# Quantising the output weights inside the loop of the first FFN product instead of after it (selective scan and ternary FFN, 8 cores)

## Chip, cores and metric

One Trainium2 chip, 8 cores. Each core runs the same program on one of the 8 batch elements, and the cores exchange nothing. The metric is device time in microseconds (us) of the slowest core; lower is better.

## What is computed

Per batch element (sequence S = 2048, width D = 2048, hidden width H = 8192), cut to what matters:

```python
x = layernorm(x + selective_scan_ffn(x, ...))
# ternary ("bit") FFN
h  = x * rsqrt(mean(x*x) + EPS) * w_norm
gv = act_quant(h) @ weight_quant(w_gv).T          # w_gv: 2*H x D
value, gate = split(gv)
u  = value * silu(gate)
out = act_quant(u) @ weight_quant(w_out).T        # w_out: D x H
x = layernorm(x + (x + out))

def weight_quant(w):                              # ternary: -1, 0, 1
    scale = 1.0 / max(mean(abs(w)), EPS)
    return clip(round(w * scale), -1, 1) / scale
def act_quant(x):                                 # 8 bits, one scale for each token
    scale = 127 / max(max(abs(x), axis=-1), EPS)
    return clip(round(x * scale), -128, 127) / scale
```

## The kernel before, in words

The program is a row of stages, each written as separate functions for the engines. Every compute instruction of VectorE (DVE) and ScalarE (ACT) goes through a wrapper (`SyncEng`, line 80 in the profile for all of them): it raises the engine's own semaphore (`sV` for DVE, `sA` for ACT), and the engine waits for that count before its next instruction. So each of the two engines runs strictly one instruction after the other, and all waits across engines are waits on these counts. `TOK` holds the counts, worked out ahead by loops that repeat the order of the code.

The stages, in order: the selective scan with the mean of all weights beside it; a stage that makes the quantised activations `q1`, kept in SBUF; **F1**, the product with `w_gv`; the **wo stage**, which quantises `w_out`; **F15**, which turns the running maximum `Mx` of |u| into per-token scales; then quantising `u` (`zt`, `mq`) and the product with the quantised `w_out` (line 1348).

**F1** (lines 957 to 1060) loops over j = 0..63 blocks of 128 hidden units. In step j:

- SyncE (SP) loads the value and the gate block of the weights (1 MB each, `wld`, ring of 3) a step ahead.
- ACT makes |w·s| into `wqt` and sign(w·s) into `wqs`, DVE combines them into ternary bf16 weights, `qwv` for the value block, and the same once more into `qwg` for the gate block. I call these four ACT and two DVE instructions the *quantising part*.
- TensorE (PE) multiplies: 4 slices of 512 tokens, 16 + 16 matmuls for each slice, into `pvg`. It waits for `qwg` of step j and, slice by slice, for `u` of step j-1, which frees PSUM.
- For step j-1, four times (once for each slice): DVE `gc_t` = gate·c1b, ACT `sg_t` = silu(gc_t), DVE `sg_t`·c1b, DVE `u_r` = value·sg_t, ACT `au_t` = |u_r|, DVE `Mx` = max(Mx, au_t). I call it the *epilogue*. After the fourth, ACT issues the store of `u_r` (1 MB, `u_sp`) on its own DMA queue.

**The wo stage** (lines 1062 to 1110) starts when F1 has ended. 128 units of 128x1024 weights: SP loads `wo_r` (512 KB, 2 buffers), ACT makes |w·s| and sign(w·s) into the first halves of `wqt` and `wqs`, DVE combines them into `qo_t` (2 buffers), ACT issues the store of unit i-1 to `qo_sp` (256 KB). The next unit's first ACT instruction waits for the DVE instruction of this one, since `wqt` is single.

After it F15 begins on DVE with a copy `trt` from `Mx`. The loads of `u_sp` by GpSimd (POOL) and of `qo_sp` by SP further on wait for the stores.

Of the kernel before, what the change touches and what calls it, by code (L numbers as in the profile page):

```python
# [86 lines left out]
def build_program(upto="F2", dbg=()):  # L87
    stage_n = STAGES.index(upto) - 4
    nc = bass.Bass("TRN2", target_bir_lowering=False)
# [15 lines left out]
    woutT = nc.dram_tensor("woutT", [2, HC, 128, 8 * 128], F32, kind="ExternalInput").ap()  # L105
# [4 lines left out]
    qo_sp = nc.dram_tensor("qo_sp", [2, HC // 4, 128, 4 * 1024], BF16, kind="Internal").ap()  # L110
# [789 lines left out]
    u_r = fsb(nc.sbuf_tensor("u_r", [128, 2 * S], F32))  # L900
    gc_t = fsb(nc.sbuf_tensor("gc_t", [128, TS], F32))
    sg_t = fsb(nc.sbuf_tensor("sg_t", [128, TS], F32))
    au_t = fsb(nc.sbuf_tensor("au_t", [128, TS], F32))
    wo_r = fsb(nc.sbuf_tensor("wo_r", [128, 2 * 1024], F32))
    qo_t = fsb(nc.sbuf_tensor("qo_t", [128, 2 * 1024], BF16))
    f1p = contextlib.ExitStack()
    pvg = f1p.enter_context(nc.psum_tensor("pvg", [128, 8 * TS], F32))

# [15 lines left out]
    for j in range(HC + 1):  # L924
        if j < HC:
            a += 2; TOK[("qv", j)] = a
            a += 2; TOK[("qg", j)] = a
        if j >= 1:
            jj = j - 1
            for ts in range(NTS):  # L930
                a += 1; TOK[("silu", jj, ts)] = a
                a += 1; TOK[("au", jj, ts)] = a
            _usp_cnt[jj % 2] += 16
            TOK[("usp", jj)] = (rUSP.sems[jj % 2].h, _usp_cnt[jj % 2])
    for j in range(HC + 1):
        if j < HC:
            v_ += 1; TOK[("ternv", j)] = v_
            v_ += 1; TOK[("terng", j)] = v_
        if j >= 1:
            jj = j - 1  # L940
            for ts in range(NTS):
                v_ += 1; TOK[("gc", jj, ts)] = v_
                v_ += 1; TOK[("sg2", jj, ts)] = v_
                v_ += 1; TOK[("u", jj, ts)] = v_
                v_ += 1; TOK[("mx", jj, ts)] = v_
    for j in range(HC):
        for ts in range(NTS):
            m += 1
            TOK[("mm", j, ts)] = m
# [21 lines left out]
    @SCA  # L971
    def _(sc):
        sc.wait_ge(sA.h, tok_w0done)
        for j in range(HC + 1):
            if j < HC:
                sc.wait_ge(*TOK[("ldv", j)])
                if j >= 1:
                    sc.wait_ge(sV.h, TOK[("terng", j - 1)])
                sc.activation(out=wqt[:], in_=wld[:, (2 * j % 3) * 2048:(2 * j % 3 + 1) * 2048],
                              func=AF.Abs, scale=sgv128[:])  # L980
                sc.activation(out=wqs[:], in_=wld[:, (2 * j % 3) * 2048:(2 * j % 3 + 1) * 2048],
                                     func=AF.Sign, scale=sgv128[:])
                sc.wait_ge(*TOK[("ldg", j)])
                sc.wait_ge(sV.h, TOK[("ternv", j)])
                sc.activation(out=wqt[:], in_=wld[:, ((2 * j + 1) % 3) * 2048:((2 * j + 1) % 3 + 1) * 2048],
                              func=AF.Abs, scale=sgv128[:])
                sc.activation(out=wqs[:], in_=wld[:, ((2 * j + 1) % 3) * 2048:((2 * j + 1) % 3 + 1) * 2048],
                                     func=AF.Sign, scale=sgv128[:])
            if j >= 1:
                jj = j - 1  # L990
                r = jj % 2
                for ts in range(NTS):
                    sc.wait_ge(sV.h, TOK[("gc", jj, ts)])
                    sc.activation(out=sg_t[:], in_=gc_t[:], func=AF.Silu)
                    sc.wait_ge(sV.h, TOK[("u", jj, ts)])
                    sc.activation(out=au_t[:],
                                         in_=u_r[:, r * S + ts * TS:r * S + (ts + 1) * TS],
                                         func=AF.Abs)
                sc.wait_ge(sV.h, TOK[("mx", jj, NTS - 1)])
                rUSP.inc(jj, sc.dma_start(out=u_sp[jj], in_=u_r[:, r * S:(r + 1) * S]))  # L1000
    assert sA.n == end_a

    @VEC
    def _(v):
        for j in range(HC + 1):
            if j < HC:
                v.wait_ge(sA.h, TOK[("qv", j)])
                if j >= 2:
                    v.wait_ge(sMM.h, TOK[("mm", j - 2, NTS - 1)])
                v.scalar_tensor_tensor(  # L1010
                    out=qwv[:, (j % 2) * 2048:(j % 2 + 1) * 2048], in0=wqt[:],
                    scalar=0.5, in1=wqs[:], op0=ALU.is_ge, op1=ALU.mult)
                v.wait_ge(sA.h, TOK[("qg", j)])
                v.scalar_tensor_tensor(
                    out=qwg[:, (j % 2) * 2048:(j % 2 + 1) * 2048], in0=wqt[:],
                    scalar=0.5, in1=wqs[:], op0=ALU.is_ge, op1=ALU.mult)
            if j >= 1:
                jj = j - 1
                r = jj % 2
                for ts in range(NTS):  # L1020
                    q = (jj * NTS + ts) % 4
                    v.wait_ge(sMM.h, TOK[("mm", jj, ts)])
                    v.tensor_mul(out=gc_t[:],
                                 in0=pvg[:, (2 * q + 1) * TS:(2 * q + 2) * TS],
                                 in1=c1b[:, ts * TS:(ts + 1) * TS])
                    v.wait_ge(sA.h, TOK[("silu", jj, ts)])
                    v.tensor_mul(out=sg_t[:], in0=sg_t[:],
                                 in1=c1b[:, ts * TS:(ts + 1) * TS])
                    if jj >= 2:
                        v.wait_ge(*TOK[("usp", jj - 2)])  # L1030
# [43 lines left out]
    @SCA
    def _(sc):
        for i in range(2 * HC + 1):
            if i < 2 * HC:
                sc.wait_ge(rWO.sems[i % 2].h, 16 * (i // 2 + 1))
                if i == 0:
                    sc.wait_ge(sV.h, wo_v0)  # L1080
                else:
                    sc.wait_ge(sV.h, wo_v0 + i)
                sc.activation(out=wqt[:, 0:1024],
                              in_=wo_r[:, (i % 2) * 1024:(i % 2 + 1) * 1024],
                              func=AF.Abs, scale=sout128[:])
                sc.activation(out=wqs[:, 0:1024],
                              in_=wo_r[:, (i % 2) * 1024:(i % 2 + 1) * 1024],
                              func=AF.Sign, scale=sout128[:])
            if i >= 1:
                ii = i - 1  # L1090
                dg, j = divmod(ii, HC)
                sc.wait_ge(sV.h, wo_v0 + ii + 1)
                rQoS.inc(ii, sc.dma_start(
                    out=qo_sp[dg, j // 4, :, (j % 4) * 1024:(j % 4 + 1) * 1024],
                    in_=qo_t[:, (ii % 2) * 1024:(ii % 2 + 1) * 1024]))
    tok_woq = sA.n

    @VEC
    def _(v):
        for i in range(2 * HC):  # L1100
            v.wait_ge(sA.h, wo_a0 + 2 * (i + 1))
            if i >= 2:
                v.wait_ge(rQoS.sems[i % 2].h, 16 * (i // 2))
            v.scalar_tensor_tensor(out=qo_t[:, (i % 2) * 1024:(i % 2 + 1) * 1024],
                                   in0=wqt[:, 0:1024], scalar=0.5,
                                   in1=wqs[:, 0:1024], op0=ALU.is_ge, op1=ALU.mult)
    tok_qodone = sV.n
# [466 lines left out]
```

## Time and profile before

| | us |
|---|---|
| median of 2 runs (7633.83 and 7651.46) | 7642.64 |
| the profiled execution, its time | 7636.9 |
| its span on the slowest core (core 0) | 7635.3 |
| spans of all cores | 7598.5 to 7635.3 |
| busy in that span: PE, DVE, ACT, POOL | 3231.7, 4178.1, 3082.2, 247.8 |
| mean granted TensorE clock, cores 0 to 7 | 0.697 to 0.701 |

The profile covers one execution, on its slowest core. "PE" is TensorE's matmuls, "SPq", "ACTq" and "POOLq" are the parts of an engine that issue DMAs. Times inside it are counted from the span's start.

### The profile page before, as it was taken

What the parts mean: (1) busy time and instruction counts of PE and PEld (TensorE: products, weight loads), DVE (VectorE), ACT (ScalarE), POOL (GpSimd) and SP (SyncE); (2) the same over time, 40 slices, a digit from 0 to 9 for tenths busy, and PEclk for the clock granted to TensorE, in tenths of its full rate; (3) what the DMA queues carried; (4) which work ended last, traced back from release to release, by engine and by line L of the source; (5) the groups of instructions that cost most, each with busy time, mean ns of one, the idle gap of its engine ahead of it and who ended that gap; (6) DMA issues with size and microseconds to landing.
All of it is one profiled execution on the core that took longest, in us unless ns stands there. A gap on an engine that the chain in (4) does not pass through costs nothing.

```text
span 7635.3 us, 48837 instructions; the slowest of 8 cores (7598.5 to 7635.3 us)
## 1 busy us (share of the span) xinstructions
PE 3231.7 (42%) x12882; PEld 1326.2 (17%) x13138; DVE 4178.1 (55%) x3305; ACT 3082.2 (40%) x2971; POOL 247.8 (3%) x471
## 2 busy tenths in 40 slices
PE   2200202102088888888888100000540714426186
PEld 0000000000033333333333000000220202112032
DVE  3845374665844444444444334677776576576612
ACT  2520212122143443344333554566565465465501
POOL 2011000000000000000000000000000000000000
PEclk8555555555599999999999555555775857668577
DMA  8998200001032222222222565111434415325233
GB/s 187 318 332 257 70 14 31 22 22 41 0 110 94 100 94 94 94 100 94 94 94 89 172 197 165 50 59 63 152 109 137 135 52 176 94 99 165 67 121 110
DMA packets 217459, 853.69 MB, mean 112 GB/s; under 512 B 34656, under 2 KB 34656, under 8 KB 159840
## 3 DMA queue, kind: packets, MB, share of 16 engines
q1 hardware_dynamic: 101808, 503.38, 20.2%
q0 software_dynamic: 50864, 179.37, 8.3%
q10 hardware_dynamic: 64512, 167.80, 5.9%
q8 instruction: 108, 1.77, 0.1%
q14 instruction: 167, 1.37, 0.1%
HBM read 694.24 MB, written 167.77 MB: 113 GB/s over the span
## 4 chain that ended last, share of the span: by engine, by line
DVE 49%; ACT 18%; DMA 14%; PE 7%; issue 7%; ACTq 2%; POOL 2%; DVEq 1%; POOLq 0%; SPq 0%
DVE zt L80 16%; DMA ub<-u_sp 5%; ACT wqt L80 5%; ACT wqs L80 5%; DVE res L80 3%; DVE paby L80 3%; PE pout L1348 3%; DMA wmean<-wgvt 3%; DVE Mx L80 3%; DVE sg_t L80 2%; DVE gc_t L80 2%; DVE u_r L80 2%; DMA wo_r<-woutT 2%; ACT sg_t L80 2%; ACT au_t L80 2%
## 5 line engine op out<-in xcount | busy, mean ns | idle before, releaser
L1348 PE MATMUL pout<-q_r,qo_r 128*128 128x512 bf16 x4012 | 935.4, 394 | 1127.4 <-DMA qo_r<-qo_sp 588.7
L1050 PE MATMUL pvg<-q,qwv 128*128 128x512 bf16 x4014 | 1025.4, 410 | 381.2 <-DVE u_r L80 215.9
L80 DVE SCALAR_TENSOR_TENSOR zt<-mq,zt 128x1024 f32<-128x1024 f32 x896 | 1098.7, 1226 | 160.4 <-DVE zt L80 158.2
L80 ACT ACTIVATE mq<-zt,pbh 128x1024 f32<-128x1024 f32 x896 | 1028.8, 1148 | 229.8 <-DVE zt L80 226.7
L1055 PE MATMUL pvg<-q,qwg 128*128 128x512 bf16 x4014 | 919.9, 379 | 4.3
L80 ACT ACT_TABLE_LOAD x82 | 105.2, 1283 | 1712.0 <-DVE q L80 404.3
L1348 PEld LDWEIGHTS pout<-q_r,qo_r 128*128 128x128 bf16 x4096 | 410.9, 101 | 1656.2 <-issue 1257.9
L1050 PEld LDWEIGHTS pvg<-q,qwv 128*128 128x128 bf16 x4096 | 422.6, 104 | 954.5 <-issue 547.8
L1055 PEld LDWEIGHTS pvg<-q,qwg 128*128 128x128 bf16 x4096 | 400.8, 98 | 483.3
L80 DVE TENSOR_TENSOR ub<-ub,s2b 128x1024 f32<-128x1024 f32 x128 | 156.9, 1225 | 435.4 <-DMA ub<-u_sp 434.5
L80 ACT ACTIVATE sg_t<-gc_t 128x512 f32<-128x512 f32 x256 | 161.2, 630 | 552.4 <-DVE gc_t L80 552.4
L80 ACT ACTIVATE wqt<-wld,sgv 128x2048 f32<-128x2048 f32 x128 | 256.3, 2002 | 251.7 <-DVE qwv L80 164.6
L80 DVE SCALAR_TENSOR_TENSOR qo_t<-wqt,wqs 128x1024 bf16<-128x1024 f32 x128 | 156.9, 1226 | 354.5 <-ACT wqs L80 332.7
L80 ACT ACTIVATE au_t<-u_r 128x512 f32<-128x512 f32 x256 | 161.2, 630 | 469.5 <-DVE u_r L80 469.5
L80 DVE TENSOR_REDUCE accW<-wmean 128x1 f32<-128x2048 f32 (+1 forms) x128 | 224.4, 1753 | 212.2 <-DMA wmean<-wgvt 144.8
L1233 POOL DMA_DIRECT2D ub<-u_sp x256 | 136.2, 536 | 6242.0 <-ACT c2b L80 4024.9
L80 DVE SCALAR_TENSOR_TENSOR qwv<-wqt,wqs 128x2048 bf16<-128x2048 f32 x64 | 146.7, 2293 | 313.8 <-ACT wqs L80 308.9
L80 ACT ACTIVATE wabs<-wmean 128x2048 f32<-128x2048 f32 (+1 forms) x128 | 189.9, 1483 | 283.1 <-DMA wmean<-woutT 204.7
L1448 PE MATMUL pout<-o_ts,onesc 128*1 128x512 f32 x128 | 63.9, 663 | 567.6 <-DVE o_ts L80 567.6
L80 ACT ACTIVATE mq<-ub,pbh 128x1024 f32<-128x1024 f32 x128 | 147.0, 1148 | 378.2 <-DVE ub L80 377.0
L80 DVE SCALAR_TENSOR_TENSOR qwg<-wqt,wqs 128x2048 bf16<-128x2048 f32 x64 | 146.7, 2292 | 275.3 <-ACT wqs L80 275.3
L80 DVE TENSOR_TENSOR Mx<-Mx,au_t 128x512 f32<-128x512 f32 x256 | 177.2, 692 | 212.7 <-ACT au_t L80 212.7
(147 smaller groups left out, 3682.1 us busy)
## 6 DMA issues: line engine op xcount, KB each, us to landing
wld<-wgvt SPq DMA_DIRECT2D x128, 1024.0 KB, 5.5
qo_r<-qo_sp SPq DMA_DIRECT2D x128, 1024.0 KB, 5.7
wmean<-wgvt SPq DMA_DIRECT2D x64, 1024.0 KB, 7.6
wmean<-wgvt POOLq DMA_DIRECT2D x64, 1024.0 KB, 11.3
u_sp<-u_r ACTq DMA_DIRECT2D x64, 1024.0 KB, 4.1
wo_r<-woutT SPq DMA_DIRECT2D x128, 512.0 KB, 3.8
ub<-u_sp POOLq DMA_DIRECT2D x256, 256.0 KB, 5.5
wmean<-woutT SPq DMA_DIRECT2D x64, 512.0 KB, 12.8
```

What stands on the lines that cost most here:

```text
L80: r = f(*a, **kw)
L1050: t.matmul(pvg[:, 2 * q * TS:(2 * q + 1) * TS], qwv[:, r * 2048 + k * 128:r * 2048 + (k + 1) * 128], q1[:, (ts * DC + k) * TS:(ts * DC + k ...
L1055: last = t.matmul(pvg[:, (2 * q + 1) * TS:(2 * q + 2) * TS], qwg[:, r * 2048 + k * 128:r * 2048 + (k + 1) * 128], q1[:, (ts * DC + k) * TS ...
L1233: tk = rUB.inc(u, g.dma_start(out=ub2[:, (2 * lane + half) * TS:(2 * lane + half + 1) * TS], in_=u_sp[2 * u + half, :, ts * TS:(ts + 1) * ...
L1348: last = t.matmul(pout[:, d * TS:(d + 1) * TS], qo_r[:, base + d * 128:base + (d + 1) * 128], rhs, start=(j == 0), stop=(j == HC - 1))
L1448: sMM.inc(t.matmul(pout[0:1, 0:TS], onesc[:], o_ts[:, d * TS:(d + 1) * TS], start=(d == 0), stop=(d == DC - 1)))
```

## The change

The wo stage as a stage of its own is gone. Its 128 units now run inside F1's loop, two per step, behind the epilogue (and in step 0, where there is no epilogue, behind the quantising part). `au_t` is dropped: |u| is written into `gc_t`, whose silu has been taken by then. The freed room and more goes to `woqt` and `woqs`, the units' own buffers for |w·s| and the sign. The loads of `wo_r` move from SP to GpSimd. On ACT the store of unit i-2 is issued ahead of unit i; the last two stores follow the last epilogue. The waits now go by `TOK`.

```diff
-    au_t = fsb(nc.sbuf_tensor("au_t", [128, TS], F32))
     wo_r = fsb(nc.sbuf_tensor("wo_r", [128, 2 * 1024], F32))
     qo_t = fsb(nc.sbuf_tensor("qo_t", [128, 2 * 1024], BF16))
+    woqt = fsb(nc.sbuf_tensor("woqt", [128, 1024], F32))
+    woqs = fsb(nc.sbuf_tensor("woqs", [128, 1024], BF16))
...
@@ ACT, loop over j, in the epilogue
-                    sc.activation(out=au_t[:],
+                    sc.activation(out=gc_t[:],
                                          in_=u_r[:, r * S + ts * TS:r * S + (ts + 1) * TS],
                                          func=AF.Abs)
                 sc.wait_ge(sV.h, TOK[("mx", jj, NTS - 1)])
                 rUSP.inc(jj, sc.dma_start(out=u_sp[jj], in_=u_r[:, r * S:(r + 1) * S]))
+            for h in ((0, 1) if j < HC else ()):
+                i = 2 * j + h
+                wl = i % 2
+                if i >= 2:
+                    sc.wait_ge(sV.h, TOK[("wot", i - 2)])
+                    dgp, jwp = divmod(i - 2, HC)
+                    rQoS.inc(i - 2, sc.dma_start(
+                        out=qo_sp[dgp, jwp // 4, :, (jwp % 4) * 1024:(jwp % 4 + 1) * 1024],
+                        in_=qo_t[:, wl * 1024:(wl + 1) * 1024]))
+                sc.wait_ge(rWO.sems[wl].h, 16 * (i // 2 + 1))
+                if i >= 1:
+                    sc.wait_ge(sV.h, TOK[("wot", i - 1)])
+                sc.activation(out=woqt[:],
+                              in_=wo_r[:, wl * 1024:(wl + 1) * 1024],
+                              func=AF.Abs, scale=sout128[:])
+                sc.activation(out=woqs[:],
+                              in_=wo_r[:, wl * 1024:(wl + 1) * 1024],
+                              func=AF.Sign, scale=sout128[:])
+            if j == HC:
+                for i in (2 * HC - 2, 2 * HC - 1):
...
@@ DVE, loop over j
                     v.tensor_max(out=Mx[:, ts * TS:(ts + 1) * TS],
-                                 in0=Mx[:, ts * TS:(ts + 1) * TS], in1=au_t[:])
+                                 in0=Mx[:, ts * TS:(ts + 1) * TS], in1=gc_t[:])
+            for h in ((0, 1) if j < HC else ()):
+                i = 2 * j + h
+                wl = i % 2
+                v.wait_ge(sA.h, TOK[("woq", i)])
+                if i >= 2:
+                    v.wait_ge(rQoS.sems[wl].h, 16 * (i // 2))
+                v.scalar_tensor_tensor(out=qo_t[:, wl * 1024:(wl + 1) * 1024],
+                                       in0=woqt[:], scalar=0.5, in1=woqs[:],
+                                       op0=ALU.is_ge, op1=ALU.mult)
...
-    wo_a0 = sA.n
-    wo_v0 = sV.n
-
-    @blk.sync
-    def _(s):
+    @blk.gpsimd
+    def _(g):
         for i in range(2 * HC):
-            if i >= 2:
-                s.wait_ge(sV.h, wo_v0 + (i - 1))
-            dg, j = divmod(i, HC)
-            rWO.inc(i, s.dma_start(out=wo_r[:, (i % 2) * 1024:(i % 2 + 1) * 1024],
-                                   in_=woutT[dg, j]))
...
+            if i < 2:
+                g.wait_ge(sV.h, pP_v)
+                g.wait_ge(sA.h, pP_a)
+                g.wait_ge(sLn1.h, tok_ln1_all)
+            else:
+                g.wait_ge(sA.h, TOK[("woq", i - 2)])
+            dg, jw = divmod(i, HC)
+            rWO.inc(i, g.dma_start(out=wo_r[:, (i % 2) * 1024:(i % 2 + 1) * 1024],
+                                   in_=woutT[dg, jw]))
```

Left out is the removed code of the wo stage on ACT and DVE, which is told in words above.

ACT before, end of an F1 step and start of the next (the DMA is the store of `u_r`):

```order
L80 ACTIVATE sg_t<-gc_t 128x512 [waits sA,sV]
L80 ACTIVATE au_t<-u_r 128x512 [waits sA,sV]
L1000 DMA u_sp<-u_r 128x2048 [waits sA,sV]
L80 ACTIVATE wqt<-wld,sgv 128x2048 [waits rWLD0,sV]
L80 ACTIVATE wqs<-wld,sgv 128x2048 [waits sA]
```

ACT now, at the same place (`rWO` are the semaphores of the `wo_r` loads):

```order
L80 ACTIVATE sg_t<-gc_t 128x512 [waits sA,sV]
L80 ACTIVATE gc_t<-u_r 128x512 [waits sA,sV]
L1007 DMA u_sp<-u_r 128x2048 [waits sA,sV]
L1014 DMA qo_sp<-qo_t 128x1024 [waits sV]
L80 ACTIVATE woqt<-wo_r,sout 128x1024 [waits rWO0,sV]
L80 ACTIVATE woqs<-wo_r,sout 128x1024 [waits sA]
L1014 DMA qo_sp<-qo_t 128x1024 [waits sA,sV]
L80 ACTIVATE woqt<-wo_r,sout 128x1024 [waits rWO1,sV]
L80 ACTIVATE woqs<-wo_r,sout 128x1024 [waits sA]
L80 ACTIVATE wqt<-wld,sgv 128x2048 [waits sA,rWLD2,sV]
```

Four activations and two stores stand between the store of `u_r` and the next quantising part; the first `qo_sp` store is directly behind the `u_sp` store on the same queue.

DVE before, the same place:

```order
L80 TENSOR_TENSOR u_r<-pvg,sg_t 128x512 [waits sV,rUSP1,sA]
L80 TENSOR_TENSOR Mx<-Mx,au_t 128x512 [waits sV,sA]
L80 SCALAR_TENSOR_TENSOR qwv<-wqt,wqs 128x2048 [waits sV,sA,sMM]
L80 SCALAR_TENSOR_TENSOR qwg<-wqt,wqs 128x2048 [waits sV,sA]
L80 TENSOR_TENSOR gc_t<-pvg,c1b 128x512 [waits sV,sMM]
```

DVE now (`rQoS` are the semaphores of the `qo_sp` stores):

```order
L80 TENSOR_TENSOR u_r<-pvg,sg_t 128x512 [waits sV,rUSP0,sA]
L80 TENSOR_TENSOR Mx<-Mx,gc_t 128x512 [waits sV,sA]
L80 SCALAR_TENSOR_TENSOR qo_t<-woqt,woqs 128x1024 [waits sV,sA,rQoS0]
L80 SCALAR_TENSOR_TENSOR qo_t<-woqt,woqs 128x1024 [waits sV,sA,rQoS1]
L80 SCALAR_TENSOR_TENSOR qwv<-wqt,wqs 128x2048 [waits sV,sA,sMM]
L80 SCALAR_TENSOR_TENSOR qwg<-wqt,wqs 128x2048 [waits sV,sA]
L80 TENSOR_TENSOR gc_t<-pvg,c1b 128x512 [waits sV,sMM]
```

Two DVE instructions were put in, each with a wait for the store of the unit that used its half of `qo_t` before.

## Rows read from the trace of the kernel before

**Rows 1.** F1 and wo stage: us, then PE, PEld, DVE, ACT, POOL busy, PEclk, DMA, GB/s

```profile
2102.00:4152.00 2050.00, 1812.04 (x7752) 795.75 (x7912) 964.04 (x1102) 809.35 (x740) 0.00 (x0) 0.94 0.27 97
4232.00:4742.00 510.00, 0.00 (x0) 0.00 (x0) 157.12 (x129) 293.69 (x257) 0.00 (x0) 0.50 0.63 196
```

**Rows 2.** Chain of waits over one step of F1 (start us, us, what)

```profile
3016.53 0.70 DVE Mx L80
3017.30 0.33 ACTq L1000
...
3017.79 2.01 ACT wqt L80
...
3031.11 0.70 DVE gc_t L80
...
3035.94 0.70 DVE gc_t L80
...
3049.92 0.70 DVE Mx L80
```

**Rows 3.** First quantising instruction of steps 2 and 63, timeline of ACT

```profile
2155.99 2.00 ACT L80 ACTIVATE wqt<-wld,sgv 128x2048 f32<-128x2048 f32 x1 [1.36 <-DVE Mx L80]
...
4178.05 2.00 ACT L80 ACTIVATE wqt<-wld,sgv 128x2048 f32<-128x2048 f32 x1 [1.36 <-DVE Mx L80]
```

**Rows 4.** The wo stage's two ends, timeline

```profile
4229.51 0.69 DVE L80 TENSOR_TENSOR Mx<-Mx,au_t 128x512 f32<-128x512 f32 x1 [0.82 <-ACT au_t L80]
...
4741.79 1.22 DVE L80 COPY trt<-Mx 64x2048 f32<-64x2048 f32 x1 [0.17 <-DVE qo_t L80]
```

**Rows 5.** One unit of the wo stage, timeline

```profile
4255.68 1.15 ACT L80 ACTIVATE wqt<-wo_r,sout 128x1024 f32<-128x1024 f32 x1 [1.49 <-DVE qo_t L80]
4256.92 1.15 ACT L80 ACTIVATE wqs<-wo_r,sout 128x1024 bf16<-128x1024 f32 x1
...
4258.24 1.23 DVE L80 SCALAR_TENSOR_TENSOR qo_t<-wqt,wqs 128x1024 bf16<-128x1024 f32 x1 [2.65 <-ACT wqs L80]
4259.56 1.15 ACT L80 ACTIVATE wqt<-wo_r,sout 128x1024 f32<-128x1024 f32 x1 [1.49 <-DVE qo_t L80]
```

**Rows 6.** DMA issues of the page: engine, count, KB each, median us to landing

```profile
wmean<-wgvt POOLq DMA_DIRECT2D x64, 1024.0 KB, 11.3
u_sp<-u_r ACTq DMA_DIRECT2D x64, 1024.0 KB, 4.1
```

**Rows 7.** DMA traffic 3017 to 3023 us (one `u_sp` store), in 40 slices

```profile
GB/s 0 0 0 0 0 0 0 492 382 382 492 382 492 273 601 273 601 55 819 0 765 109 655 218 0 0 0 0 0 0 0 0 0 0 0 0 0 0 0 0
```

**Rows 8.** DMA traffic 4740 to 4748 us (two `qo_sp` stores), in 40 slices

```profile
GB/s 0 0 0 0 0 51 338 389 399 133 0 0 102 410 369 369 62 0 0 0 0 0 0 0 0 0 0 0 0 0 0 0 0 0 0 0 0 0 0 0
qo_sp<-qo_t ACTq DMA_DIRECT2D x2, 256.0 KB, 2.4
```

**Rows 9.** Sixteen 256 KB stores in a row on ACT's queue, timeline

```profile
891.79 9.98 ACTq L716 DMA_DIRECT2D ln_sp<-res  x16
```

**Rows 10.** `qo_t` and its stores, 4599 to 4612 us: DMA to landing

```profile
DMA to landing us min/median/max: 3.8/4.0/4.0
```

**Rows 11.** Step 0 and 1 of F1 on ACT, timeline

```profile
2117.17 2.00 ACT L80 ACTIVATE wqs<-wld,sgv 128x2048 bf16<-128x2048 f32 x1
2121.66 2.00 ACT L80 ACTIVATE wqt<-wld,sgv 128x2048 f32<-128x2048 f32 x1 [2.49 <-DVE qwg L80]
...
2145.35 0.63 ACT L80 ACTIVATE sg_t<-gc_t 128x512 f32<-128x512 f32 x1 [1.75 <-DVE gc_t L80]
...
2151.68 0.63 ACT L80 ACTIVATE sg_t<-gc_t 128x512 f32<-128x512 f32 x1 [3.39 <-DVE gc_t L80]
```

**Rows 12.** PE in F1 and after a long idle stretch, timeline

```profile
2238.12 6.42 PE L1050 MATMUL pvg<-q,qwv 128*128 128x512 bf16 x16 [4.45 <-DVE u_r L80]
...
3016.85 3.62 PE L1050 MATMUL pvg<-q,qwv 128*128 128x512 bf16 x16
...
5630.16 29.57 PE L1348 MATMUL pout<-q_r,qo_r 128*128 128x512 bf16 x126 [149.62 <-ACT o_ts L80]
```

More of the change, by code:

```diff
@@ L934, in build_program @@
             TOK[("usp", jj)] = (rUSP.sems[jj % 2].h, _usp_cnt[jj % 2])
+        if j < HC:
+            for h in (0, 1):
+                a += 2; TOK[("woq", 2 * j + h)] = a
     for j in range(HC + 1):
@@ L945, in build_program @@
                 v_ += 1; TOK[("mx", jj, ts)] = v_
+        if j < HC:
+            v_ += 1; TOK[("wot", 2 * j)] = v_
+            v_ += 1; TOK[("wot", 2 * j + 1)] = v_
     for j in range(HC):
@@ L1000, in _ @@
                 rUSP.inc(jj, sc.dma_start(out=u_sp[jj], in_=u_r[:, r * S:(r + 1) * S]))
+            for h in ((0, 1) if j < HC else ()):
[19 more added lines that the diff above has]
+                    wl = i % 2
+                    sc.wait_ge(sV.h, TOK[("wot", i)])
+                    dgp, jwp = divmod(i, HC)
+                    rQoS.inc(i, sc.dma_start(
+                        out=qo_sp[dgp, jwp // 4, :, (jwp % 4) * 1024:(jwp % 4 + 1) * 1024],
+                        in_=qo_t[:, wl * 1024:(wl + 1) * 1024]))
     assert sA.n == end_a
@@ L1036, in _ @@
                     v.tensor_max(out=Mx[:, ts * TS:(ts + 1) * TS],
-                                 in0=Mx[:, ts * TS:(ts + 1) * TS], in1=au_t[:])
+                                 in0=Mx[:, ts * TS:(ts + 1) * TS], in1=gc_t[:])
+            for h in ((0, 1) if j < HC else ()):
+                i = 2 * j + h
+                wl = i % 2
+                v.wait_ge(sA.h, TOK[("woq", i)])
[4 more added lines that the diff above has]
+                                       op0=ALU.is_ge, op1=ALU.mult)
     assert sV.n == end_v
@@ L1060, in build_program @@
     assert sMM.n == end_m
-    wo_a0 = sA.n
-    wo_v0 = sV.n
-    @blk.sync
-    def _(s):
+    @blk.gpsimd
+    def _(g):
         for i in range(2 * HC):
-            if i >= 2:
-                s.wait_ge(sV.h, wo_v0 + (i - 1))
-            dg, j = divmod(i, HC)
-            rWO.inc(i, s.dma_start(out=wo_r[:, (i % 2) * 1024:(i % 2 + 1) * 1024],
-                                   in_=woutT[dg, j]))
[L1074 to L1107, printed above, removed]
+            if i < 2:
[7 more added lines that the diff above has]
+                                   in_=woutT[dg, jw]))
+    tok_woq = end_a
+    tok_qodone = end_v
     tok_qosp = [s.tok() for s in rQoS.sems]
```

## Prediction

> **What bounds the kernel now.** I read first how busy each engine is by stage [rows 1]. In F1 no engine is full: of 2050 us PE works 1812, DVE 964 and ACT 809. DVE and ACT together make 1773, so the question is whether they ever work side by side. The chain of waits over one step says that they don't: the step goes from the end of `Mx` at 3016.53 + 0.69 = 3017.22 over the store's issue to `wqt` at 3017.79, and then in turns between ACT and DVE through the quantising part up to 3031.1 and through four epilogues of about 4.83 us each (3031.11 to 3035.94) to the next `Mx` at 3049.92 [rows 2]. PE is not in it. From step 2 to step 63 the first `wqt` moves from 2155.99 to 4178.05, 61 steps, or 33.15 us a step [rows 3]. So F1 is bounded by one chain of ACT and DVE in turns; all that is put into it lengthens it.
>
> The wo stage is such a chain too. PE does nothing there, and of 510 us ACT works 294 and DVE 157 [rows 1]. A unit starts with ACT at 4255.68, its sign at 4256.92, DVE at 4258.24, and the next unit's ACT at 4259.56: 3.88 us [rows 5]. From the last `Mx` of F1 (4229.51 + 0.69 = 4230.20) to the first copy of F15 at 4741.79 it is 511.6 us for 128 units, 4.0 each [rows 4].
>
> **What is removed.** F15 starts 0.17 us behind the last DVE instruction of F1 instead of behind the last unit [rows 4]. That takes 511.6 - 0.2 = 511.4 us away. What comes later (F15, the quantising of `u`, the second product) has the same work. The last two `qo_sp` stores are issued right ahead of F15 as they were before, so what waits for them further on waits for nothing new.
>
> **What is put into the step.** The units stand between the epilogue and the next quantising part on both engines, so they are on the chain, and PE's idle time doesn't help, since PE was never what they waited for. I follow one step from `Mx`'s end at 3017.22, with the durations of rows 5.
>
> 1. The `u_sp` store is issued at 3017.30 for 0.33 us as before [rows 2]. The `qo_sp` store of unit i-2 follows. Sixteen stores in a row took 9.98 us to issue, 0.62 each [rows 9]; I take 0.5, between 0.33 for one alone and that. ACT starts the first unit at 3018.3 instead of 3017.79.
> 2. DVE could start 2.56 us later (4255.68 to 4258.24 [rows 5]), at 3020.86.
> 3. But DVE now also waits for the `qo_sp` store just issued, as it will overwrite that half of `qo_t`. That is the term which the change doesn't show. Alone it would be there in time: 2.4 us to landing [rows 8], so 3017.7 + 2.4 = 3020.1. Yet it stands behind 1 MB of `u_sp` on one queue. The traffic of such a store begins 0.75 us after the issue and lasts until about 3020.6 (slices 8 to 24 of 0.15 us, 3018.05 to 3020.6 [rows 7]), and it lands 4.1 us after issue, at 3021.4 [rows 6]. The 256 KB behind it need some 0.7 us more: the first of two such stores filled about four slices of 0.2 us [rows 8], and 16 in a row took 0.62 each [rows 9]. Both have the same 0.8 us from the last byte to landing (rows 6 and 7: 3021.4 less 3020.6). So it lands at about 3022.1, and DVE starts at 3022.15, a wait of 1.3 us.
> 4. ACT's second unit starts 1.32 us after DVE did (4258.24 to 4259.56 [rows 5]), at 3023.47. Its store was issued right behind the first sign, and has landed before it is asked for. ACT goes on to `wqt` of the next step after twice 1.24 us (4255.68 to 4256.92 [rows 5]), at 3025.95. It doesn't wait for DVE here, for `woqt` and `woqs` are buffers of their own, and DVE's second 1.23 us lie beside the 4.2 us of `wqt` and `wqs`.
>
> The step grows by 3025.95 - 3017.79 = 8.16 us. Without the wait in 3 it would be 1.29 less, 6.87.
>
> A rule of the Trainium skill speaks to this wait (DMA: Bandwidth & Descriptors, "Queues, rings and completion order"): descriptors of a queue are consumed in ring order on each DMA engine, and the write that raises the semaphore lands only after all earlier writes of that engine. By it the small store can't overtake the large one and the wait stands; a store that overtook it would give the 6.87 above. No row of before has a `qo_sp` store behind a `u_sp` store, so the trace doesn't decide it.
>
> **The first and the last step.** In step 0 the two units stand behind the quantising part: the last sign starts at 2117.17 and is over at about 2119.26, then abs and sign, DVE at 2121.8, the second pair from 2123.1, and step 1 starts at 2125.6 instead of 2121.66 [rows 11], 4.0 late. The first epilogue there lost some 1.6 us to PE (ACT idle 3.39 ahead of the `sg_t` at 2151.68, against 1.75 a slice earlier [rows 11]), which falls away: +2.4. In step 63 no quantising part follows, and DVE's second unit comes onto the chain: it starts 2.56 after 3023.47 and ends 1.4 later with its gap, so the next `gc_t` comes at 3027.43 instead of 3017.39: +10.0.
>
> **Sum.** 62 × 8.16 + 2.4 + 10.0 - 511.4 = 505.9 + 12.4 - 511.4 = +6.9 us. From the profiled execution, 7636.9, that is 7644 us, against a median of 7642.64 for the runs shown: no change.
>
> **What I cost at nothing, and its cover.** `gc_t` in the place of `au_t` adds no wait: on both engines the reader is through before the next writer, by the engine's own order. GpSimd has nothing else to do in F1 [rows 1]; its load of unit i+2 is issued when ACT is through with unit i, and is wanted a step later, over 33 us, while loads of twice the size from there took 11.3 us in the crowded first stage [rows 6]. If that cover went, ACT would stand still at the head of a unit. PE has 8 groups of 16 matmuls a step, at most 3.62 us each [rows 12], 29.0 us, in a step that grows to 41.3. It may start slower after the longer idle time, and I bound this from both sides: nothing, as in the group of 3.62, and 2.8 us, as in the group of 6.42 behind 4.45 us idle. Behind 149.6 us idle, 126 matmuls took 29.57 us, where 7.9 groups of 3.62 are 28.5, about 1 us more [rows 12]. All that stays below 32, so PE isn't on the chain.
>
> **Rivals.**
>
> *A: the small store isn't held up* (by the large one, or since engines that finish early serve it first). For it: only the receipt at the end is shared. Against: the DMA slices are full of the large store until 3020.6 [rows 7], and both are on one queue. A step grows by 6.87, and 63 steps give back 81 us: 7563.
>
> *B, slower: the small store starts only when the large one has landed, or lands late.* The place is DVE's wait for `rQoS` in front of the first unit. For it: where the stage was crowded, such a store took 4.0 us instead of 2.4 [rows 10]. Against: 16 in a row kept the queue going at 0.62 us each [rows 9]. With landing at 3021.4 + 2.4 = 3023.8 DVE starts 1.7 us later than I say, 63 × 1.7 = 107 us: 7751. With 3021.4 + 4.0 = 3025.4 it is 3.3 us, 208 us: 7852. From any delay on the result is on the slower side, as the forecast sum is just above zero, and it is over 2% from 2.3 us of delay on (146 us over 63 steps).
>
> *C: PE falls behind since it stays at its lower level.* At 1.2 instead of 2.4 GHz a step of PE is 58 us, more than 41.3, and F1 would end 62 × (58 - 41.3) = 1035 us later than by my sum: some 8680. It decides from where PE needs over 41.3 us, with some 40% of its matmuls at the lower level. For it: the granted clock was 0.94 of full in F1 with 4 us idle a step (2050 - 1812 over 62 steps, rows 1), and now there are 11. Against: after 149.6 us idle the loss was 1 us and then over [rows 12]. The Trainium skill warns of it (TensorE: Matmul & The Clock Gate, "HAM oscillation"): idle stretches between bursts make each burst start throttled. That rule and the row agree on a cost for each burst; by it C would not come, as each burst here is 128 matmuls long.
>
> *D: the units cost less than rows 5 say*, 5.6 us or less a step, over 2% faster. The chain of four ACT and one DVE instruction alone is 2.56 + 1.32 + 2.48 = 6.36 us [rows 5], so almost nothing is for it.
>
> **Chances.** My forecast 0.60 (its own range 7612 to 7676, from 0.5 us of error a step either way); A 0.20; B 0.15, a third of it over 2%; C 0.03; D 0.02. The predicted time is 7644. The range reaches to A and to the nearer end of B: 7560 to 7750. 2%, about what a measurement of this kernel can tell from no change, is 153 us. Faster by over 2%: 0.03. Slower: 0.05 from B and 0.03 from C, 0.08. Within: 0.89.
>
> **What would show it.** In the new profile: the distance between two first `wqt` is 41.3 us from step 2 on; in the waits DVE `qo_t` is released by the DMA `qo_sp<-qo_t` once a step, with about 1.3 us behind ACT's sign; the `qo_sp` stores have two kinds of landing, some 4.4 and some 2.4 us; no ACT instruction waits for `wo_r`; PE's idle time in front of a step is some 11 us and its first group 5 to 6.5; F15 starts 0.2 us behind the last `Mx`, at about 4749. I am wrong in the main term if DVE starts the first unit before 3.8 us or after 6 us past `Mx`'s end, and wrong in kind if PE or a `wo_r` load ends a wait in F1.

## The result and the profile after

The changed kernel takes 7664.36 us (median of 33 runs, 7626.77 to 7707.91), the kernel before beside it 7633.3 us (32 runs). The ratio is 1.0041, 95% interval 1.0027 to 1.0055: about 31 us slower, within 2%. Forecast were +7 us and no change.

The profiled execution's slowest core is core 5, with a span of 7684.7 us; the others range from 7605.0 to 7677.2. The places of [rows 3] and [rows 4], in the timeline of that core (start us, us, engine, line, operation; in brackets the idle time before and what ended it):

```profile
2102.07 2.00 ACT L80 ACTIVATE wqt<-wld,sgv 128x2048 f32<-128x2048 f32 x1
2160.11 2.00 ACT L80 ACTIVATE wqt<-wld,sgv 128x2048 f32<-128x2048 f32 x1 [0.20 <-ACT woqs L80]
4707.45 2.00 ACT L80 ACTIVATE wqt<-wld,sgv 128x2048 f32<-128x2048 f32 x1 [0.20 <-ACT woqs L80]
4769.08 0.69 DVE L80 TENSOR_TENSOR Mx<-Mx,gc_t 128x512 f32<-128x512 f32 x1 [0.82 <-ACT gc_t L80]
4769.94 1.22 DVE L80 COPY trt<-Mx 64x2048 f32<-64x2048 f32 x1 [0.17 <-DVE Mx L80]
```

The wo stage is gone: `trt` starts 0.17 us behind the last `Mx`, where it was 511.6 us [rows 4]. Steps 2 to 63 now take (4707.45 - 2160.11) / 61 = 41.76 us each, against 33.15 [rows 3]: 8.61 more. Where the 8.61 go is seen in one step, the stretch of [rows 2]:

```profile
3030.00 0.69 DVE L80 TENSOR_TENSOR Mx<-Mx,gc_t 128x512 f32<-128x512 f32 x1 [0.83 <-ACT gc_t L80]
...
3030.77 0.33 ACTq L1007 DMA_DIRECT2D u_sp<-u_r  x1
3031.18 0.40 ACTq L1014 DMA_DIRECT2D qo_sp<-qo_t  x1
3031.74 1.15 ACT L80 ACTIVATE woqt<-wo_r,sout 128x1024 f32<-128x1024 f32 x1 [1.84 <-issue]
3032.98 1.15 ACT L80 ACTIVATE woqs<-wo_r,sout 128x1024 bf16<-128x1024 f32 x1
...
3034.26 0.33 ACTq L1014 DMA_DIRECT2D qo_sp<-qo_t  x1
...
3035.80 1.22 DVE L80 SCALAR_TENSOR_TENSOR qo_t<-woqt,woqs 128x1024 bf16<-128x1024 f32 x1 [5.11 <-DMA qo_sp<-qo_t]
...
3037.12 1.15 ACT L80 ACTIVATE woqt<-wo_r,sout 128x1024 f32<-128x1024 f32 x1 [3.00 <-DVE qo_t L80]
3038.36 1.15 ACT L80 ACTIVATE woqs<-wo_r,sout 128x1024 bf16<-128x1024 f32 x1
3039.68 1.23 DVE L80 SCALAR_TENSOR_TENSOR qo_t<-woqt,woqs 128x1024 bf16<-128x1024 f32 x1 [2.66 <-ACT woqs L80]
3039.71 2.00 ACT L80 ACTIVATE wqt<-wld,sgv 128x2048 f32<-128x2048 f32 x1 [0.20 <-ACT woqs L80]
```

The sign of the first unit ends at 3034.13, but DVE starts at 3035.80, when the store issued at 3031.18 has landed. The second unit's DVE instruction lies beside `wqt`, and no ACT instruction waits for a `wo_r` load. The waits of DVE for `qo_t`, over the whole program (us in total, times), and the landing of the `qo_sp` stores:

```profile
  DMA qo_sp<-qo_t: 330.1, 63
  ACT woqs L80: 170.4, 65
...
DMA to landing us min/median/max: 2.3/4.4/6.2
```

The median landing is over two kinds of store: those directly behind `u_sp` land 4.5 us after their issue, the others 2.8 (medians of each kind). The 330.1 us are the whole idle time from the last `Mx` to the start of the first unit's DVE instruction, 63 times 5.24 us (5.07 in the median step, 6.75 in the longest). And PE, in the rows that answer to [rows 12]:

```profile
3056.32 6.56 PE L1092 MATMUL pvg<-q,qwv 128*128 128x512 bf16 x16 [12.19 <-DVE u_r L80]
```

It stands idle for 12.19 us ahead of a step, where it was 4.45 in [rows 12], and its first group of 16 is slow as it was there: the granted clock is 0.54 in it, nearly all at its lower level (1.2 GHz, 0.5), and 1.00 (2.4 GHz) in the group that starts at 3033.61. PE costs the chain nothing: six waits of DVE for `qwv` are put down to PE, 18.7 us in total, but they last 3.1 us each, as when ACT ends them (3.07).

### The profile page after: what moved, and what is told of

Its sections match the earlier page's. It is cut to its first block, busy times and chain, and to the rows that moved or that the text cites. A ratio compares the mean times of both kernels' runs of the same rounds, so it can differ in the third digit from the quotient of the medians.

```text
span 7684.7 us, 49097 instructions; the slowest of 8 cores (7605.0 to 7684.7 us)
## 1 busy us (share of the span) xinstructions
PE 3373.7 (44%) x13138; PEld 1353.6 (18%) x13138; DVE 4177.8 (54%) x3305; ACT 3081.0 (40%) x2970; POOL 315.4 (4%) x599
## 4 chain that ended last, share of the span: by engine, by line
DVE 49%; ACT 17%; DMA 15%; PE 8%; issue 7%; POOL 2%; ACTq 1%; DVEq 1%; POOLq 0%; SPq 0%
DVE zt L80 16%; DMA ub<-u_sp 5%; DMA qo_sp<-qo_t 4%; PE pout L1358 3%; DVE res L80 3%; ACT wqt L80 3%; ACT wqs L80 3%; DVE paby L80 3%; DMA wmean<-wgvt 3%; DVE Mx L80 3%; DVE sg_t L80 2%; DVE u_r L80 2%; DVE gc_t L80 2%; ACT sg_t L80 2%; ACT gc_t L80 2%
## 5 line engine op out<-in xcount | busy, mean ns | idle before, releaser
L1358 PE MATMUL pout<-q_r,qo_r 128*128 128x512 bf16 x4096 | 1013.7, 417 | 1086.7 <-DMA qo_r<-qo_sp 570.9
L1092 PE MATMUL pvg<-q,qwv 128*128 128x512 bf16 x4096 | 1069.4, 421 | 864.9 <-DVE u_r L80 705.5
L1097 PE MATMUL pvg<-q,qwg 128*128 128x512 bf16 x4096 | 937.1, 382 | 0.0
L1358 PEld LDWEIGHTS pout<-q_r,qo_r 128*128 128x128 bf16 x4096 | 428.2, 105 | 1676.3 <-issue 1473.7
L80 DVE SCALAR_TENSOR_TENSOR qo_t<-woqt,woqs 128x1024 bf16<-128x1024 f32 x128 | 156.9, 1226 | 500.6 <-DMA qo_sp<-qo_t 330.1
L80 ACT ACTIVATE gc_t<-u_r 128x512 f32<-128x512 f32 x256 | 161.2, 630 | 468.5 <-DVE u_r L80 468.5
L80 DVE TENSOR_TENSOR sg_t<-sg_t,c1b 128x512 f32<-128x512 f32 x256 | 177.3, 693 | 212.7 <-ACT sg_t L80 212.7
L80 DVE TENSOR_TENSOR Mx<-Mx,gc_t 128x512 f32<-128x512 f32 x256 | 177.2, 692 | 212.0 <-ACT gc_t L80 212.0
L80 ACT ACTIVATE woqt<-wo_r,sout 128x1024 f32<-128x1024 f32 x128 | 146.9, 1148 | 314.8 <-DVE qo_t L80 192.2
```

The costliest lines, as they stand in the source:

```text
L80: r = f(*a, **kw)
L1092: t.matmul(pvg[:, 2 * q * TS:(2 * q + 1) * TS], qwv[:, r * 2048 + k * 128:r * 2048 + (k + 1) * 128], q1[:, (ts * DC + k) * TS:(ts * DC + k ...
L1097: last = t.matmul(pvg[:, (2 * q + 1) * TS:(2 * q + 2) * TS], qwg[:, r * 2048 + k * 128:r * 2048 + (k + 1) * 128], q1[:, (ts * DC + k) * TS ...
L1358: last = t.matmul(pout[:, d * TS:(d + 1) * TS], qo_r[:, base + d * 128:base + (d + 1) * 128], rhs, start=(j == 0), stop=(j == HC - 1))
```

## Experiments

Ratios are to the kernel before, run beside each kernel on the same chip, with their 95% interval. The changed kernel is at 1.0041. DVE's wait for the first unit is counted from the end of the last `Mx`, 5.24 us on average in the changed kernel.

**1. The small store ahead of the large one.**

```diff
+                if j < HC:
+                    i = 2 * j
+                    sc.wait_ge(sV.h, TOK[("wot", i - 2)])
...
+                    rQoS.inc(i - 2, sc.dma_start(out=qo_sp[...], in_=qo_t[:, 0:1024]))
                 sc.wait_ge(sV.h, TOK[("mx", jj, NTS - 1)])
                 rUSP.inc(jj, sc.dma_start(out=u_sp[jj], in_=u_r[:, r * S:(r + 1) * S]))
...
-                if i >= 2:
+                if i >= 2 and h == 1:
```

> The changed kernel with one edit: the qo_sp store of unit 2j-2 is issued ahead of the u_sp store of the same step, not behind it. Theory (the small store lands late because it stands behind 1 MB on one queue): DVE's wait on it goes, DVE starts the first unit about 3.2 us after the end of Mx instead of 5.24 (mean of the changed kernel), and 63 steps give back 2.0 us each: some 128 us less than the changed kernel, 97 less than the kernel before, ratio 0.987. Rival (the store lands late in F1 wherever it stands, since the stage's traffic is heavier): the wait stays, within 20 us of the changed kernel, ratio about 1.003.

Measured: 0.9873 (0.9836 to 0.9911). The store now goes out while DVE makes `Mx` (here it lands 2.8 us after its issue), and DVE waits only for ACT, 3.18 us on average:

```profile
3026.51 0.69 DVE L80 TENSOR_TENSOR Mx<-Mx,gc_t 128x512 f32<-128x512 f32 x1 [0.82 <-ACT gc_t L80]
3026.54 0.33 ACTq L1010 DMA_DIRECT2D qo_sp<-qo_t  x1
3027.28 0.33 ACTq L1014 DMA_DIRECT2D u_sp<-u_r  x1
...
3030.33 1.22 DVE L80 SCALAR_TENSOR_TENSOR qo_t<-woqt,woqs 128x1024 bf16<-128x1024 f32 x1 [3.12 <-ACT woqs L80]
```

**2. Three parts of `qo_t` instead of two**, so that the first unit's wait is for a store of the step before. To make room, `scr3`, which only F15 uses, is allocated there.

```diff
-    rQoS = DRing(st, nc, "rQoS", 2)
+    rQoS = DRing(st, nc, "rQoS", 3)
...
-    qo_t = fsb(nc.sbuf_tensor("qo_t", [128, 2 * 1024], BF16))
+    qo_t = fsb(nc.sbuf_tensor("qo_t", [128, 3 * 1024], BF16))
...
-                if i >= 2:
-                    v.wait_ge(rQoS.sems[wl].h, 16 * (i // 2))
+                if i >= 3:
+                    v.wait_ge(rQoS.sems[i % 3].h, 16 * (i // 3))
```

> The changed kernel with qo_t as a ring of three halves (and three store semaphores), so that DVE waits for a store issued a step earlier; the order of issues stays. Theory: the wait goes, the two issues ahead of the first activation stay, DVE starts 3.6 us after Mx's end, 63 steps give back 1.6 us each: 103 us less than the changed kernel, 72 less than the kernel before, ratio 0.9905. Rival (DVE's wait only covers another one, of ACT or of a load): the time stays within 20 us of the changed kernel.

Measured: 0.9908 (0.9878 to 0.9939). DVE starts 3.64 us after `Mx` on average, with the order of issues as in the changed kernel. The wait was real, and it covered nothing else. It went although the stores of this execution landed later, not earlier: after 6.0 us on the profiled core (core 7, median of all) instead of 4.4. On core 2 it was 4.5; why the cores differ is not known.

**3. The large store from SyncE's queue.**

```diff
@@ SP, between the two weight loads of step j
+            if j >= 3:
+                s.wait_ge(sV.h, TOK[("mx", j - 3, NTS - 1)])
+                rUSP.inc(j - 3, s.dma_start(out=u_sp[j - 3], in_=u_r[...]))
...
@@ ACT
-                sc.wait_ge(sV.h, TOK[("mx", jj, NTS - 1)])
-                rUSP.inc(jj, sc.dma_start(out=u_sp[jj], in_=u_r[:, r * S:(r + 1) * S]))
```

> The changed kernel with the u_sp store issued by SyncE on its own queue; the qo_sp stores stay on ACT's. Both go at the same moment over the same 16 DMA engines. Theory (order within one queue is what holds the small store up): it lands 2.4 to 3.3 us after its issue, DVE starts 3.2 to 3.5 us after Mx's end, 110 to 128 us less than the changed kernel, ratio about 0.987 to 0.990. Rival (the engines' bandwidth is what it waits for, whichever queue): landing stays at 4.4 or more, DVE at 4.9, some 20 us less than the changed kernel, ratio 1.001.

Measured: 0.9807 (0.9762 to 0.9851), more than expected. The landing of all small stores is 3.2 us in the median instead of 4.4:

```profile
u_sp<-u_r SPq DMA_DIRECT2D x64, 1024.0 KB, 4.1
qo_sp<-qo_t ACTq DMA_DIRECT2D x128, 256.0 KB, 3.2
```

```profile
3031.95 0.69 DVE L80 TENSOR_TENSOR Mx<-Mx,gc_t 128x512 f32<-128x512 f32 x1 [0.82 <-ACT gc_t L80]
3031.98 0.33 ACTq L1020 DMA_DIRECT2D qo_sp<-qo_t  x1
3032.46 1.15 ACT L80 ACTIVATE woqt<-wo_r,sout 128x1024 f32<-128x1024 f32 x1 [0.62 <-ACT gc_t L80]
3032.72 0.33 SPq L974 DMA_DIRECT2D u_sp<-u_r  x1
...
3035.03 1.23 DVE L80 SCALAR_TENSOR_TENSOR qo_t<-woqt,woqs 128x1024 bf16<-128x1024 f32 x1 [2.38 <-ACT woqs L80]
```

What I had missed: with the store, ACT's wait for the last `Mx` goes too. So the two stores don't go at the same moment, as expected: the small one is issued at 3031.98, 0.74 us ahead of the large one, as in experiment 1, and lands 2.5 us after its issue (median of those that DVE waits for). This run therefore doesn't show what a queue of its own would do for a store issued together with the large one. ACT starts the unit at 3032.46, before `Mx` ends at 3032.64, and DVE comes 2.39 us after `Mx`. (5.24 - 2.39) × 63 = 180 us less than the changed kernel is 1.0041 - 180/7620 = 0.9805, as measured. Of the 2.85 us, 2.06 came in experiment 1 from the order alone (5.24 to 3.18); the rest is ACT's wait.

**4. The large store in two halves**, the first ten microseconds earlier.

```diff
+                    if ts == 1:
+                        rUSP.inc(jj, sc.dma_start(out=u_sp[jj, :, 0:1024],
+                                                  in_=u_r[:, r * S:r * S + 1024]))
                 sc.wait_ge(sV.h, TOK[("mx", jj, NTS - 1)])
-                rUSP.inc(jj, sc.dma_start(out=u_sp[jj], in_=u_r[:, r * S:(r + 1) * S]))
+                rUSP.inc(jj, sc.dma_start(out=u_sp[jj, :, 1024:2048],
+                                          in_=u_r[:, r * S + 1024:(r + 1) * S]))
```

> The changed kernel with the u_sp store cut in two: the first 512 KB are issued behind slice 1 of the epilogue, ten microseconds earlier, the second 512 KB where the whole was. Theory (the qo_sp store waits for the bytes ahead of it on its queue, 2.5 us for 1 MB): 512 KB less ahead of it are 1.2 us, DVE starts 4.0 us after Mx's end instead of 5.24, 63 x 1.2 = 76 us less than the changed kernel, ratio 0.994. Rival (it waits for the landing of the DMA ahead, whose cost is mostly fixed, 2.4 us even for 256 KB): about 0.6 us a step less, ratio 0.999.

Measured: 0.9941 (0.9912 to 0.9969); the wait is 252.3 us over 62 times, 4.07 us each. Half the bytes ahead, 1.17 us less. The small store lands 3.3 us after its issue (median), where 2.4 us after the landing of the half store would be 4.7.

```profile
  DMA qo_sp<-qo_t: 252.3, 62
```

**5. Both small stores behind the large one, the wanted one last.**

```diff
-                if i >= 2:
-                    sc.wait_ge(sV.h, TOK[("wot", i - 2)])
...
+                for p in ((i - 1, i - 2) if i >= 2 and h == 0 else ()):
+                    sc.wait_ge(sV.h, TOK[("wot", p)])
...
```

> The changed kernel with both qo_sp stores of the step before issued behind u_sp, unit 2j-1's ahead of unit 2j-2's, for which DVE waits: 256 KB more ahead. Theory (bytes on the queue, 0.62 us for 256 KB in a row of stores): DVE starts 5.9 us after Mx's end, 63 x 0.65 = 41 us more than the changed kernel, ratio 1.0095. Rival (each DMA ahead costs its full 2.4 us): 150 us more, ratio 1.024; or no change where the wait isn't order on the queue, 1.004.

Measured: 1.0200 (1.0151 to 1.0249). On the profiled core (3) DVE's wait is 465.6 us over 63 times, 7.39 each, 2.15 more than the 5.24 of the changed kernel, for 256 KB more ahead: far from the theory, near the rival.

```profile
3019.79 0.33 ACTq L1007 DMA_DIRECT2D u_sp<-u_r  x1
3020.20 1.38 ACTq L1014 DMA_DIRECT2D qo_sp<-qo_t  x2
3021.74 1.15 ACT L80 ACTIVATE woqt<-wo_r,sout 128x1024 f32<-128x1024 f32 x1 [2.82 <-issue]
...
3027.48 1.23 DVE L80 SCALAR_TENSOR_TENSOR qo_t<-woqt,woqs 128x1024 bf16<-128x1024 f32 x1 [7.77 <-DMA qo_sp<-qo_t]
```

The third issue in a row stood for 0.9 us on ACT's queue, and the traffic of this stretch (3019 to 3029 us, slices of 0.25 us) shows the large store at some 400 GB/s, and the small ones behind it falling to half of that and less:

```profile
GB/s 0 0 0 0 0 0 426 459 262 426 524 426 459 229 459 393 172 336 287 147 147 123 57 131 221 213 221 189 107 8 82 213 229 360 328 426 180 115 33 0
```

That slow traffic is not the price of 256 KB ahead, for not all cores of this execution have it. DVE's waits for the stores on core 0 and on core 6 (us, times, longest):

```profile
DVE qo_t L80 <- DMA qo_sp<-qo_t: 393.4, 63, 7.6
```

```profile
DVE qo_t L80 <- DMA qo_sp<-qo_t: 483.9, 63, 10.1
```

Core 0 waits 6.24 us each time, 0.88 more than core 0 of the changed kernel (338.1 us over 63 times), and core 1 is 0.61 above its own of the changed kernel: there the theory's 0.65 is about right. On these two the small stores land 4.5 to 4.9 us after their issue (medians), on the other six, with the same issues, 5.3 to 6.5. What slows them there is open.

**6. The same, the wanted one first.** Only `(i - 1, i - 2)` becomes `(i - 2, i - 1)`.

> Both qo_sp stores behind u_sp as in the run before (which came out at 1.020, not at the 1.0095 of bytes alone), but in the order 2j-2, 2j-1, so that the one DVE waits for stands first. Theory (a store waits only for what is ahead of it on its queue; the second small one costs 2 us for those behind it): DVE's wait ends as in the changed kernel, 5.24 us after Mx's end, ratio 1.004. Rival (two small stores in flight slow each other, their 2 KB pieces going out at about half the rate): the first lands late as well, DVE starts 6.5 to 7.4 us after Mx's end, ratio 1.014 to 1.020.

Measured: 1.0032 (1.0002 to 1.0062), the wait 337.7 us over 62 times, 5.45 each, not 6.5 or more. So what stands ahead counts, and what stands behind next to nothing (0.2 us). On all eight cores the small stores land after 4.5 to 4.9 us (medians), as on cores 0 and 1 of experiment 5.

**7. Both small stores ahead of the large one** (order 2j-1, 2j-2, in front of the wait for `Mx`).

> Both qo_sp stores ahead of u_sp, in the order 2j-1, 2j-2. They are issued while DVE makes the last Mx. Theory (bytes ahead on the queue): the second lands 0.65 us later than one alone, some 3.0 us after its issue, hidden behind ACT's first unit; u_sp's issue as third is held up by up to 1 us, DVE starts 3.2 to 4.1 us after Mx's end, ratio 0.987 to 0.994. Rival (two small stores slow each other also without a large one): the second lands over 4.5 us after its issue, DVE starts 4.3 us or later, ratio 0.996 or more.

Measured: 0.9871 (0.9834 to 0.9908), and DVE starts 3.49 us after `Mx` on average. The first small store lands 2.8 us after its issue, the second, issued 0.42 later, 3.2 after its own (medians of the profiled core): 0.8 us for the 256 KB ahead. With 1 MB ahead of both it is the same on core 0 of experiment 5, where the second lands 0.8 us after the first. So the price of 256 KB on the queue is 0.6 to 0.9 us here, not 2.15.

**8. One part of the change alone**: the kernel before with |u| in `gc_t`, without `au_t`.

```diff
-                    sc.activation(out=au_t[:],
+                    sc.activation(out=gc_t[:],
...
-                                 in0=Mx[:, ts * TS:(ts + 1) * TS], in1=au_t[:])
+                                 in0=Mx[:, ts * TS:(ts + 1) * TS], in1=gc_t[:])
```

> The kernel before with one part of the change: |u| is written into gc_t and au_t is gone. Theory: both engines are through with gc_t by their own order, no wait is added, ratio 1.000 (within 0.3%). Rival (the next gc_t now waits for Mx, or the silu for Abs): 0.5 us or more in each of 256 slices, 128 us, ratio 1.017.

Measured: 0.9972 (0.9944 to 1.0001), and a step takes 33.15 us as before: no cost.

**9. The units inside the epilogue.** The same instructions as in the changed kernel, each in a gap in which its engine waited for the other:

```diff
@@ ACT, in the loop over the four slices
                     sc.activation(out=sg_t[:], in_=gc_t[:], func=AF.Silu)
+                    if ts in (0, 2):
+                        sc.wait_ge(rWO.sems[wl].h, 16 * (i // 2 + 1))
...
+                        sc.activation(out=woqt[:], in_=wo_r[...], func=AF.Abs, scale=sout128[:])
                     sc.wait_ge(sV.h, TOK[("u", jj, ts)])
                     sc.activation(out=gc_t[:], in_=u_r[...], func=AF.Abs)
+                    if ts in (0, 2):
+                        sc.activation(out=woqs[:], in_=wo_r[...], func=AF.Sign, scale=sout128[:])
+                    if ts in (1, 3):
+                        sc.wait_ge(sV.h, TOK[("wot", i)])
+                        rQoS.inc(i, sc.dma_start(out=qo_sp[...], in_=qo_t[...]))
@@ DVE, behind gc_t of slices 1 and 3
+                        v.scalar_tensor_tensor(out=qo_t[...], in0=woqt[:], scalar=0.5,
+                                               in1=woqs[:], op0=ALU.is_ge, op1=ALU.mult)
```

> The changed kernel with the units inside the epilogue instead of behind it: |w.s| of a unit while ACT waits for u, the sign while ACT waits for the next gc_t, the DVE instruction behind gc_t of the next slice while ACT makes the silu; two units an epilogue, stores behind slices 1 and 3, ahead of u_sp. Theory (what costs in the changed kernel is that the units lengthen the one chain of ACT and DVE in turns, 8.6 us a step; ACT stands idle 1.75 to 1.82 us twice a slice, DVE 0.82 us twice): the four activations of 1.15 us vanish, each DVE instruction of 1.23 us sticks out of its gap by 0.5 to 0.7 us, so a step grows by 1.1 to 1.5 us: 64 x 1.3 - 511 = -428 us against the kernel before, ratio 0.944. Rival (the two engines slow each other or the semaphore waits between them add as much): a step grows by 4 us or more, ratio 0.967 or above.

Measured: 0.9444 (0.9397 to 0.9491), 7187.8 us.

```profile
3004.07 0.69 DVE L80 TENSOR_TENSOR sg_t<-sg_t,c1b 128x512 f32<-128x512 f32 x1 [0.82 <-ACT sg_t L80]
3004.17 1.15 ACT L80 ACTIVATE woqt<-wo_r,sout 128x1024 f32<-128x1024 f32 x1 [0.20 <-ACT sg_t L80]
...
3005.79 0.63 ACT L80 ACTIVATE gc_t<-u_r 128x512 f32<-128x512 f32 x1 [0.47 <-DVE u_r L80]
3006.51 1.15 ACT L80 ACTIVATE woqs<-wo_r,sout 128x1024 bf16<-128x1024 f32 x1
...
3008.17 0.63 ACT L80 ACTIVATE sg_t<-gc_t 128x512 f32<-128x512 f32 x1 [0.51 <-DVE gc_t L80]
...
3008.32 1.23 DVE L80 SCALAR_TENSOR_TENSOR qo_t<-woqt,woqs 128x1024 bf16<-128x1024 f32 x1 [0.24 <-DVE gc_t L80]
...
3009.72 0.69 DVE L80 TENSOR_TENSOR sg_t<-sg_t,c1b 128x512 f32<-128x512 f32 x1 [0.17 <-DVE qo_t L80]
```

ACT's idle time in front of |u| falls from 1.82 to 0.47 us, and in front of the silu from 1.75 to 0.51: the activations vanish there. DVE's instruction stands where it would have waited 0.82 for the silu, and sticks out. From the second `wqt` of step 2 to that of step 63 it is (4274.05 - 2149.75) / 61 = 34.82 us a step, 1.67 more than in the kernel before, where 1.1 to 1.5 was expected, and 6.9 less than in the changed one. Not all of the 6.9 is the placing: in experiment 1, where the store's wait is gone as well, a step takes 39.69 us, so 4.9 are. From the first `wqt` to F15 it is 2229.0 us, 404 less than before; the medians differ by 421, so the 428 expected was met in part by what lies outside F1.

**10. The same with the large store from SyncE's queue**, as in experiment 3.

> The interleaved kernel with the u_sp store issued by SyncE, so that ACT doesn't wait for the last Mx of an epilogue. Theory: in the run with only that edit ACT started what follows 0.75 us earlier a step than with u_sp on its queue; the same here, 62 x 0.75 = 46 us less than the interleaved kernel, ratio to the kernel before 0.938. Rival: SyncE's program has the weight loads behind that store, a load now comes late and ACT waits for wld; not faster than the interleaved kernel, ratio 0.944 or more.

Measured: 0.9374 (0.9329 to 0.942), 7142.45 us, the fastest here, faster than both kernels. A step takes 34.03 us, 0.79 less than in experiment 9. In the loop ACT never waited for `wld`.

## Why the prediction was right, point by point

- *One chain of ACT and DVE bounds F1, and all put into it lengthens it.* Shown: steps grew by 8.61 us, and the same instructions moved into the gaps of the chain took the program to 0.9444. DVE and ACT are busy as long as in the changed kernel (4177 and 3081 us); only the place of their instructions differs.
- *What is removed, 511.4 us.* Seen in the timeline. From the first `wqt` of F1 to F15 it is 4769.94 - 2102.07 = 2667.9 us, where it was 2633.3 (4741.79 less the first `wqt` at 2108.48): +34.6. The rest of the profiled difference is not F1's (the core begins F1 6.4 us earlier, and takes 21 us longer after it); the 33 runs say 31. The cores of a kernel differ among each other here by 12 to 24 us; over all eight, the mean of this stretch grows from 2644.1 to 2674.1 us, +30.0.
- *The first and the last step.* To the first `wqt` of step 2 it takes 58.04 us instead of 47.51, +10.5; forecast were 2.4 + 8.16 = 10.6. From the first `wqt` of step 63 to F15 it is 62.5 us; before, 563.7 - 511.4 = 52.3; +10.2 against 10.0.
- *The hidden term, DVE's wait for the store behind `u_sp`.* Right in kind: it goes with the order (experiments 1 and 7) or with a third buffer (2), it shrinks with the bytes ahead (4), and a store behind doesn't change it (6). The rule of the Trainium skill that I had leaned on (DMA: Bandwidth & Descriptors, "Queues, rings and completion order": descriptors of a queue are consumed in ring order) agrees with these runs: ahead of the large store the small one landed 2.8 us after its issue, directly behind it 4.5. Not shown is whether the same bytes on another queue, issued at the same moment, would hold it up as well: in experiment 3 the small store went first.
- *Its size is the step that was off.* I had DVE start 4.93 us after `Mx`'s end; it was 5.24. That is 0.31 × 63 = 20 of the 28 us missing. I had taken the landing from single stretches of a clean store; in the median step it is 5.07, and some late landings (up to 6.2 us after the issue) make the mean. The other 7 are step 4 of my list: `wqt` comes 2.59 us after the second unit's start (3037.12 to 3039.71), not twice 1.24; from the sign to `wqt` it is 1.35 us (3038.36 to 3039.71), not 1.24 as from |w·s| to the sign, 62 times. So the term that was too small is the price of a step, 8.16 for 8.61, by 5%; and the sum is the difference of two terms of over 500 us each, which such an error moves by 28.
- *Rival A* (the small store isn't held up) fell: it is what experiments 1 and 2 had to bring about, at 0.987 and 0.991. *Rival B* (it starts only when the large one has landed) fell with experiment 4 and with the 4.5 us of landing. Its other half, a late landing in a crowded stretch, was not at work in the changed kernel, but is seen on most cores of experiments 2 and 5. *Rival C* (PE falls behind) fell: PE's first group of a step took 6.56 us behind 12.19 us idle, at a granted clock of 0.54, close to the 6.42 of [rows 12], and the groups after it 3.62 again; cores with slower PE were no later in F1 (next section but one). *D* fell with 8.61.
- *Costed at nothing*: `gc_t` for `au_t` is shown by experiment 8. That the loads on GpSimd are never waited for is only seen in the traces (landing after 4.1 us, wanted over 30 us later), not tried otherwise.

## What to carry to other kernels

Moving work beside an engine that stands idle gains nothing if the work's own engines are in one chain of turns: look whose idle time it is, and put each instruction into a gap of its own engine (8.6 us a step behind the chain, under 2 inside it, for the same instructions). When a buffer is reused across a store, look at what stands ahead of that store on its queue, not at its own landing time. And when an issue is moved off an engine, the wait that it carried goes with it.

## What the runs showed of the hardware that I had not expected

- A third DMA in a row on ACT's queue behind one of 1 MB held ACT for 0.9 us at its issue (experiment 5), while the second took 0.40. With the two small ones first, these took 0.81 us together and the large one, as the third, 0.43 (experiment 7).
- Within one execution the same stores, issued alike, landed at different times on different cores: in experiment 5 the last of three after 4.8 us on core 1 and 6.5 on core 7, in experiment 2 the one behind `u_sp` after 4.5 on core 3 and 7.5 on core 7 (medians). The cause is open. A price of DMAs is better compared on several cores than read from one.
- On some cores PE ran for stretches at 4.38 us for 16 matmuls instead of 3.62, mostly on cores 6 and 7. The granted clock is 0.81 in such a stretch, between its two levels, where the group of 3.62 has 1.00. PE's waits for `u_r` are shorter by that, and F1 is no longer: from the first `wqt` to F15 it is 2673.0 us on such a core (6) and 2675.7 on one without (0). A group of core 6, and PE's waits (us, times, longest) of core 6 and of core 0, all of the changed kernel:

```profile
3020.97 4.38 PE L1097 MATMUL pvg<-q,qwg 128*128 128x512 bf16 x16
```

```profile
PE pvg L1092 <- DVE u_r L80: 599.5, 61, 13.3
```

```profile
PE pvg L1092 <- DVE u_r L80: 733.1, 62, 13.9
```
